# A three-stage transformer kernel on one core: norm sums, the residual form and the input projection in another order

## What is computed

```python
    def layer_a(x, ...):                       # on layernorm(x)
        xn = layernorm(x, in_norm_alpha, in_norm_bias)
        xz = xn @ in_proj_w.T + in_proj_b      # input projection, 256 -> 2 * 512
        x_in, z = jnp.split(xz, 2, axis=-1)
        x_conv = silu(conv1d(x_in, conv_w, 4 taps) + conv_b)
        Bm, Cm = jnp.split(x_conv @ x_proj_w.T + x_proj_b, 2, axis=-1)   # 16 states each
        delta = clip(softplus(x_conv @ dt_proj_w.T + dt_proj_b), 1e-4, 10)
        # for each row t:  h = exp(clip(delta * A, -10, 0)) * h + delta * B * x_conv
        #                  every 16th row: h scaled down where its norm is over 10
        #                  y = sum over states of C * h, + D * x_conv
        y = y * silu(z)
        return layernorm(residual + y @ out_proj_w.T + out_proj_b, ...)

    def ffn(tokens, router_w, router_b, expert_w):     # on layernorm(tokens)
        probs = softmax(tokens @ router_w.T + router_b)
        # the 6 largest of 16 are the gates, renormalized
        # out = sum over e of (tokens @ expert_w[e]) * gate[e]

    x = x + layer_a(_layernorm(x), ...)
    x = x + ffn(_layernorm(x), ...)
    x = x + layer_b(_layernorm(x), ...)
    x = x + ffn(_layernorm(x), ...)
```

## Time and profile before

| | |
|---|---|
| median of 3 runs | 4515.41 us (4514.4 to 4516.36) |
| the profiled execution | 4514.84 us, of which its span is 4512.8 us |
| mean granted TensorE clock | 0.987 |
| busy over the span | PE 94%, DVE 80%, ACT 68%, POOL 57% |
| first phase | up to about 2970 us |
| second phase | the rest; POOL does nothing in it |

### The profile page before, as it was taken

One profiled execution on the slowest core, in us unless ns is written; L12 is line 12 of the kernel. 1 busy time (PEld: TensorE's weight loads), 2 busy tenths in 40 slices (PEclk: granted clock), 3 DMA queues, 4 the chain that ended last, 5 costly groups with the idle time before them and its releaser, 6 DMA issues.

```text
span 4512.8 us, 79944 instructions
## 1 busy us (share of the span) xinstructions
PE 4253.3 (94%) x22592; PEld 2960.7 (66%) x22592; DVE 3632.4 (80%) x9610; ACT 3057.9 (68%) x8912; POOL 2588.5 (57%) x1284
## 2 busy tenths in 40 slices
PE   5899999999999999999999999988999999999999
PEld 4777777777777777777777777644444444444444
DVE  3899999999999999999999999855656657566666
ACT  5898888888888888888888888834333332333321
POOL 3988888888888888888888888930000000000000
PEclk8999999999999999999999999999999999999999
DMA  2111111111111111111111111100000000000000
GB/s 101 58 51 62 49 58 53 57 54 57 54 57 54 57 54 57 54 57 54 56 53 54 54 56 55 55 30 22 6 16 16 6 16 6 16 16 7 6 7 10
DMA packets 91560, 187.49 MB, mean 42 GB/s; under 512 B 16160, under 2 KB 58016, under 8 KB 90912
## 3 DMA queue, kind: packets, MB, share of 16 engines
q1 hardware_dynamic: 90272, 180.78, 12.2%
q10 hardware_dynamic: 1152, 5.14, 0.3%
HBM read 168.05 MB, written 17.83 MB: 41 GB/s over the span
## 4 chain that ended last, share of the span: by engine, by line
PE 49%; issue 19%; DVE 18%; POOL 11%; ACT 2%; DVEq 1%; POOLq 0%; DMA 0%; SPq 0%; ACTq 0%
PE ps L684 24%; POOL prod L331 6%; DVE macc L1004 6%; PE ps L658 4%; PE ps L808 3%; POOL hb L339 3%; PE ps L736 2%; PE ps L730 2%; PE ps L750 2%; PE ps L773 2%; PE ps L790 2%; POOL xcv L355 1%; DVE dtt L1189 1%; PE ps_dA L808 1%; PE ps L758 1%
## 5 line engine op out<-in xcount | busy, mean ns | idle before, releaser
L684 PE MATMUL ps<-w_x,mxT 128*128 128x512 f32 x4096 | 1933.7, 601 | 69.6 <-DVE macc L1004 69.6
L1004 DVE SCALAR_TENSOR_TENSOR macc<-ps,gate,macc 128x256 f32<-128x256 f32 x2048 | 977.6, 477 | 498.0 <-PE ps L684 410.0
L915 DVE TENSOR_TENSOR_SCAN hb<-ps_dA,hb 128x1088 f32<-128x1088 f32 x512 | 1240.7, 2423 | 107.4 <-POOL hb L339 99.1
L331 POOL TENSOR_TENSOR prod<-hb,cbc 128x1024 f32<-128x1024 f32 x512 | 1123.1, 2194 | 248.9 <-DVE hb L934 243.5
L339 POOL TENSOR_TENSOR hb<-u,bbc 128x1024 f32<-128x1024 f32 x512 | 1202.0, 2348 | 75.1 <-POOL prod L331 70.9
L394 ACT ACTIVATE zr<-dt,aneg 128x128 f32<-128x128 f32 x4096 | 1240.8, 388 | 1.3 <-DVE dt L1078 1.0
L684 PEld LDWEIGHTS ps<-w_x,mxT 128*128 128x128 f32 x4096 | 727.5, 191 | 739.3 <-issue 604.0
L658 PEld LDWEIGHTS ps<-prod,ident 128*128 128x128 f32 x8192 | 947.5, 192 | 151.9 <-POOL prod L331 91.4
L658 PE MATMUL ps<-prod,ident 128*128 128x128 f32 x8192 | 965.4, 276 | 41.0 <-POOL prod L331 41.0
L403 ACT ACTIVATE ps_dA<-zr 128x1024 f32<-128x1024 f32 x512 | 518.3, 1012 | 0.0
L410 ACT ACTIVATE sq<-hb 128x64 f32<-128x64 f32 x512 | 157.9, 308 | 219.9 <-DVE hb L915 217.4
(11 more groups left out here) (193 smaller groups left out, 4848.3 us busy)
## 6 DMA issues: line engine op xcount, KB each, us to landing
bbc<-bcd SPq DMA_DIRECT2D x128, 512.0 KB, 3.8
cbc<-bcd SPq DMA_DIRECT2D x128, 512.0 KB, 3.7
xt<-in_x SPq DMA_DIRECT2D x128, 128.0 KB, 3.6
x2d<-macc SPq DMA_DIRECT2D x64, 128.0 KB, 1.7
out_dram<-macc SPq DMA_DIRECT2D x64, 128.0 KB, 1.7
w_x<-in_w_x ACTq DMA_DIRECT2D x1, 4096.0 KB, 12.6
hb<-x2d SPq DMA_DIRECT2D x32, 128.0 KB, 2.4
sz<-x2d SPq DMA_DIRECT2D x16, 128.0 KB, 2.2
```

Source lines behind the costliest of these rows:

```text
L331: TT(dst, states, cc, ALU.mult).then_inc(M["prodp"], 1)
L684: last = mm(banks[p % len(banks)][:], mxT[k][:, j, :], w_x[:, j, p * 512:(p + 1) * 512], start=(j == 0), stop=(j == KD - 1))
L915: V.tensor_tensor_scan(states, dA, states, 0.0, ALU.mult, ALU.add).then_inc(M["scan"], 1)
L1004: STT(macc[k][:], banks[(e // 2) % len(banks)][:, (e % 2) * D:(e % 2 + 1) * D], gate[k][:, e:e + 1], macc[k][:], ALU.mult, ALU.add).then_i ...
```

## The change

Instructions keep their operands; some stand at another place of their engine's queue. There are five moves in the first phase:
- DVE chunk 0: the second part of the router's statistics (`mmv` and the negative mean) goes behind `dt` and `oo`.
- DVE chunk 1: the norm sums go ahead of `yg`.
- DVE chunk 3: the norm sums go between `lgt` and its maximum.
- PE: the transposes of `xn` go from chunk 1 to chunk 0, ahead of `sum_states` 3; the first half of the input projection goes from chunk 2 to chunk 1, behind the route transposes.
- ACT: the two copies to `xnT` go from chunk 1 to chunk 0, behind `route_norm` and ahead of the six decays.

In the second phase the split functions are called one after the other, so that nothing moves there.

```diff
--- before
+++ after
@@ ACT, step
+                    if c == 0 and F:
+                        a.wait_ge(M["xnT"], AHEAD + i + 3)
+                        a.wait_ge(M["z"], AHEAD + i + 2)
+                        for j in range(KD):
+                            act(xnT[:, j, :], F0[:, j * P:(j + 1) * P], ACT.Identity, bias=be_in[:, j:j + 1],
+                                scale=ga_in[:, j:j + 1]).then_inc(M["xnTs"], 1)
...
@@ PE, step
+                    if c == 0 and F:
+                        pe.wait_ge(M["xn"], AHEAD + i + 3)
+                        pe.wait_ge(M["dtb"], AHEAD + (i + 2) * EB)
...
@@ DVE, step
                 halfway(0)
                 if X_:
                     v.wait_ge(M["x1"], AHEAD + i - 1)
-                    route_norm1(i - 2, x1b[k][:])
+                    route_norm0(i - 2, x1b[k][:])
...
                     STT(oo[:], xt[1][:], r1b[1 - k][:], ob_row[:], ALU.mult, ALU.add).then_inc(M["o1"], 1)
+                if X_:
+                    route_norm1(i - 2)
                 end(0)
...
                 start(1)
+                halfway(1)
                 if B:
...
-                halfway(1)
                 end(1)
...
                 start(3)
                 if X_:
-                    route_scores(i - 2, k, F1)
+                    route_logits(i - 2, F1)
                 halfway(3)
+                if X_:
+                    route_scores(i - 2)
```

More of the change, by code:

```diff
@@ L518, in step @@
                                 act(history, ends, ACT.Identity, scale=carry[:, bass.ds(kept, 1)]).then_inc(M["carry"], 1)
[L519 to L523, removed]
                         if X_:
@@ L713, in step @@
                         transposes(c - 1)
+                    if c == 0 and F:
+                        pe.wait_ge(M["xn"], AHEAD + i + 3)
+                        pe.wait_ge(M["dtb"], AHEAD + (i + 2) * EB)
+                        for j in range(KD):
+                            last = nc.tensor.transpose(F0[:, j * P:(j + 1) * P], xn[:, j * P:(j + 1) * P], ident[:])
+                        last.then_inc(M["xnT"], 1)
                     if c == 0 and B:
@@ L716, in step @@
                     if c == 1:
[L717 to L722, removed]
                         if X_:
@@ L725, in step @@
                             route(i - 2, k, F1)
[L726 to L731, removed]
                         if F:
@@ L738, in step @@
                             last.then_inc(M["xi"], 1)
+                    if c == 2:
+                        if B:
+                            pe.wait_ge(M["yg"], AHEAD + i)
+                            for e in range(EB):
+                                last = mm(YP[:, 0:D], yg[:, e, :], w_out[:, e, :], start=(e == 0), stop=(e == EB - 1))
+                            last.then_inc(M["op"], 1)
                         if X_:
@@ L934, in bound, with route_norm0, route_norm1 @@
                 STT(last, factor, 1.0, last, ALU.min, ALU.mult).then_inc(M["hs"], 1)
-            def route_norm1(n, x):
+            def route_norm0(n, x):
                 V.bn_stats(mst[:], x).then_inc(R["st"], 1)
+            def route_norm1(n):
                 v.wait_ge(R["st"], AHEAD + n + 1)
@@ L1308, in slot @@
                         v.wait_ge(A["x3"], AHEAD + r + 1)
-                        route_norm1(r + NTILES, x3_rows(r))
+                        route_norm0(r + NTILES, x3_rows(r))
+                        route_norm1(r + NTILES)
                     if p == 5:
-                        route_scores(r + NTILES, r % 2, M0)
+                        route_logits(r + NTILES, M0)
+                        route_scores(r + NTILES)
                     if p >= 6:
```

3 lines of the change are left out of this document (2 added, 1 removed).

## The result

| | before | after |
|---|---|---|
| median of 20 runs, same chip | 4514.38 us (4507.98 to 4516.36) | 4522.55 us (4518.5 to 4526.54) |
| ratio | | 1.0019, 95% interval 1.0012 to 1.0025 |
| span of the profiled execution | 4512.8 us | 4521.7 us |
| from one tile to the next, mean of ten tiles between 1000 and 1500 us | 45.47 us | 45.60 us |

The change makes the kernel 8.2 us slower, 0.19%, and the interval lies clear of no change. The forecast was 4526.8, which is 11.4 above the median that was known then. The direction and the mechanism held, and the effect is smaller than was said by about a quarter.

What follows compares the result with a forecast made beforehand. It took the POOL–DVE chain, not busy PE, as the bound. +0.33 (chunk 0) − 0.14 (chunk 3) = +0.19 us a tile, times 60 tiles, +11.4 us on 4515.41, gave 4526.8 us; range 4513 to 4543.

Steps and rivals of the forecast that it cites:

- `dt` is held by POOL: DVE chunk 0: `dt` stands until POOL's `hb` of chunk 1 ends, finishing 0.27 to 0.29 us after it whenever issued.
- Rival 1: DVE chunk 0: `dt` is not held and runs early, so the kernel is faster, −0.25 us a tile, 4500 us; chance 0.07.
- The bound of chunk 0, +0.33: DVE chunk 0: with `mmv` and its negative behind `oo`, the bound and POOL's chain after it come 0.33 us later.
- ACT behind `mmv`: ACT: L424 1.31 us later, `mxn` 2.01 later, scan of chunk 2 0.7 later but not on the chain.
- L1107's wait for `w_out`: DVE, written L1100 in the prediction: a new 0.48 us wait for PE's `w_out`, replacing the old one for `macc`.
- The tie at the scan of chunk 3: DVE chunk 3: POOL's `hb` and DVE's own work allow the scan almost together, 0.33 to 0.38 us later; 0.33 taken.
- rival 3: PE's new wait decides the scan of chunk 3: clearly slower, +0.29 to +0.49 us a tile, 4533 to 4545 us; chance 0.20.
- Chunk 3, −0.14: DVE chunk 3: norm sums fill L950's 0.16 us wait for `lgt`, saving 0.14, so its bound is only 0.19 later.
- Chunks 4 to 7: The convolution comes 0.62 us later, hidden by 0.17 us before POOL's `prod` 4; ACT's lateness is swallowed at the tile's end.
- The sum: +0.33 − 0.14 = +0.19 us a tile over 60 tiles, +11.4 us, giving 4526.8 us, 0.25% slower.
- rival 2: No change: the pair behind `oo` costs under 0.33, chunk 3 gives 0.16; +0.02 to +0.14 a tile, 4517 to 4524 us; chance 0.28.
- The swap of chunk 1: Chunk 1: norm sums ahead of `yg` remove ACT's 0.39 us wait, which ACT's late square takes back nearly three times.

Runs made afterwards that it cites:

- after_half: The changed kernel with POOL's `hb` of chunk 1 writing only half its columns in the loop's tiles (not the same computation); 4484.57 us in one run.
- after_projfirst: The changed kernel with PE's input projection ahead of the route transposes instead of behind them; 4523.42 us, ratio 1.0017 to the kernel before.
- only_proj: The kernel before with only PE's two moves and ACT's copies to `xnT`, DVE as before; 4514.14 us, ratio 1.0.
- only_c1: The kernel before with only the norm sums of chunk 1 moved ahead of `yg`; 4514.51 us, ratio 1.0002.
- bound_first: The changed kernel with `mmv` and its negative put back ahead, then chunk 0's bound, `oo` and `dt` in that order; 4603.15 us, ratio 1.0181 to before.

## Why the prediction was right, and where it was off

**`dt` is held by POOL.** Right, and the whole case rests on it. It ended 0.29 us behind POOL's `hb` after an earlier issue, as before; after_half shows the cause. Rival 1, −0.25 us a tile, is out.

**The bound of chunk 0, +0.33.** This is the term that was too large: it is +0.28. It is so in both tiles of the loop's body, for different reasons (means of ten tiles each, 1000 to 1910 us).

In the tile that the prediction read, `mmv` did come 0.40 behind `oo`, but the negative mean came 0.20 behind it and the bound 0.07 behind that, where I had 0.22 and 0.11. Both prices were taken from the earlier trace rows, where the two stood ahead of `dt`. The last one was the distance from a small instruction to `dt`, and a distance belongs to a pair of instructions, not to the first of them.

In the other tile the premise itself fails, that the pair costs nothing ahead of `dt` and that `dt` ends where it did. There `dt` ended 0.37 us behind POOL before and ends 0.28 behind it now, so moving the pair gave back 0.08 to 0.09. Behind `oo` the pair costs 0.36 there, since the negative mean comes 0.29 behind `mmv` (1531.99 against 1531.70). The two make +0.28 again. That the one tile stood well for both is luck.

Times 60 the 0.05 makes 3 of the 4.3 us by which the forecast was high. The median of before makes another 1.0: it was 4515.41 with three runs and is 4514.38 with twenty.

**ACT behind `mmv`.** L424 was to be 1.31 later and was 1.29; `mxn` was to be 2.01 later and was 1.89 (means of ten tiles of the kind that was read). The scan of chunk 2 was to be 0.7 later and was 0.4 to 0.5. It had room, as said.

**PE.** Over 1 us of wait for `mxn`: 1.57. L1107's wait for `w_out`: 0.48 said, 0.45 seen. The tie at the scan of chunk 3 is there, and took 0.27 where 0.33 to 0.38 was said, by the smaller term of chunk 0. That PE decides nothing (against rival 3) is shown by after_projfirst and only_proj.

**Chunk 3, −0.14.** It is −0.16 and −0.13 in the two tiles of the body, and −0.15 us a tile alone.

**Chunks 4 to 7.** The convolution is later by 0.4 to 0.5, not 0.62, and hidden as said.

**The sum.** +0.28 − 0.15 = +0.13 us a tile where +0.19 was said. That is inside what rival 2 gave (+0.02 to +0.14). Rival 2's reason, that the pair behind `oo` costs less than 0.33, holds in one tile of the body (0.27) and not in the other (0.36, of which 0.08 come back). The change is slower, by an amount that sits on the edge of 0.2%. A sum of two terms of opposite sign, each good to 0.05 us, cannot say on which side of such an edge it falls, and the time came out just on the other side from the one forecast. The chances should have been nearer to even between the two.

**The swap of chunk 1** gains nothing: ACT's wait for the norm sums was not on the chain. I had counted it as a gain that ACT's lateness takes back; only_c1 shows that without the lateness there is none either.

## What to carry to other kernels

A row that is long for its size may be an engine that stands. Compare the same instruction elsewhere in the trace, and see whether its end follows another engine's end by a fixed distance. What is queued ahead of such an instruction is free as long as it stands anyway, which has to be read in every tile of a loop's body (0.66 us in one, 0.43 in the other here). What is moved behind it, ahead of a signal that another engine waits for, costs its full length. So the signal goes first and the held work into the other engine's gap, but only as far as it still fits there: one step too far (bound_first) turned −29 into +89 us.
